# Three edits in an eight-core transformer and state-space kernel: a separate cast, eight weight pieces in a visit, scale factors made per tile

## What is computed

```python
# scan part: x is [2048, 1024] on each core, d_inner 2048, 16 states
xp, z = jnp.split(x @ W_in, 2, axis=-1)
dlt, Bm, Cm = jnp.split(xp @ W_xproj, [64, 80], axis=-1)
delta = jnp.clip(softplus(dlt @ W_dt + b_dt), 0.001, 0.1)
# for every step t: h = (1 + A*dt) * h + (B*dt) * x_t ;  y_t = sum_state(C * h)
y = (scan(xp, delta, A, Bm, Cm) + D * xp) * silu(z)
x = layernorm(x + y @ W_out)
# feed-forward: int8 levels per row for activations, ternary weights
scale_w = 1 / clip(mean(abs(w)), 1e-5);  wq = clip(round(w*scale_w), -1, 1) / scale_w
scale_x = 127 / clip(max(abs(x), axis=-1), 1e-5);  xq = clip(round(x*scale_x), -128, 127) / scale_x
x = layernorm(x + bitlinear(silu(bitlinear(x, w_gate)) * bitlinear(x, w_up), w_down))
```

## Time and profile before

| | |
|---|---|
| runs shown | 9471.68 and 9613.43 us, median 9542.56 |
| the profiled execution | 9519.5 us |
| its span, slowest core (core 2) | 9517.9 us |
| spans of the 8 cores | 9418.7 (core 5) to 9517.9 us |
| VectorE busy | 6221.3 us, 65% of the span |
| TensorE busy | 3550.9 us, 37% |
| ScalarE busy | 1872.1 us, 20% |
| DMA, mean over the span | 68 GB/s |

### The profile page before, as it was taken

The page is one execution under the profiler, slowest core; times in us unless marked ns, Lnnn a source line. Parts: engine busy times, 40 slices in busy tenths (PEclk is TensorE's granted clock), DMA queues, the critical chain, the costliest instruction groups (busy, mean ns, idle before and its releaser), DMA issues.

```text
span 9517.9 us, 48227 instructions; the slowest of 8 cores (9418.7 to 9517.9 us)
## 1 busy us (share of the span) xinstructions
PE 3550.9 (37%) x13683; PEld 1381.4 (15%) x13683; DVE 6221.3 (65%) x4766; ACT 1872.1 (20%) x2102; POOL 0.2 (0%) x4
## 2 busy tenths in 40 slices
PE   6766656999943111111111111100005555222222
PEld 3211112334311000000000000000002222111011
DVE  2555553222144999998879999997774444777776
ACT  0222322111112212112222122211102222111111
POOL 0000000000000000000000000000000000000000
PEclk9655557899865555555555555555557777655556
DMA  3000012111143233333232222222331111000000
GB/s 91 5 0 0 0 40 103 66 54 71 45 157 101 94 91 90 95 84 93 90 99 91 86 82 86 86 84 88 106 120 71 71 71 70 26 27 22 22 27 22
DMA packets 238263, 648.93 MB, mean 68 GB/s; under 512 B 31419, under 2 KB 97196, under 8 KB 230644
## 3 DMA queue, kind: packets, MB, share of 16 engines
q1 hardware_dynamic: 238004, 645.86, 20.6%
HBM read 582.58 MB, written 63.18 MB: 68 GB/s over the span
## 4 chain that ended last, share of the span: by engine, by line
DVE 50%; PE 24%; issue 11%; DMA 7%; ACT 6%; SPq 1%; DVEq 1%; ACTq 0%
DVE b_sl L1219 12%; DVE b_sl L1232 6%; DVE b_sl L1207 6%; DVE qd2B L1444 5%; PE p_hB L694 5%; PE p_eoB L725 4%; DVE ternB L1440 3%; PE p_gA L1665 2%; PE p_uA L1670 2%; DVE rb L443 2%; ACT attbuf L438 2%; DVE zbuf L432 2%; DVE qdD L1444 1%; PE p_mmA L332 1%; PE p_z L447 1%
## 5 line engine op out<-in xcount | busy, mean ns | idle before, releaser
L1219 DVE TENSOR_TENSOR_SCAN b_sl<-a_sl,h_state,b_sl 128x1024 f32<-128x1024 f32 x512 | 1175.8, 2338 | 36.2 <-ACT a_sl L1199 8.8
L1199 ACT ACTIVATE a_sl<-dt_ch,A_all 128x1024 f32<-128x1024 f32 x512 | 559.9, 1140 | 2351.1 <-DVE b_sl L1219 2325.1
L1270 PE MATMUL p_aoC<-wob,ybf 128*128 128x512 bf16 x512 | 167.2, 474 | 1867.8 <-DVE ybf L1251 1769.1
L1232 DVE TENSOR_TENSOR b_sl<-b_sl,bcb 128x2048 f32<-128x2048 f32 x256 | 586.8, 2292 | 28.9 <-DVE h_state L1226 3.2
L1239 DVE TENSOR_TENSOR y_ch<-y_ch,b_sl 128x2048 f32<-128x2048 f32 x256 | 586.8, 2292 | 27.6 <-DVE b_sl L1232 1.4
L1207 DVE TENSOR_TENSOR b_sl<-dxp_ch,bcb 128x2048 f32<-128x2048 f32 x256 | 585.2, 2286 | 18.0 <-DMA bcb<-bc_scr 17.3
L1125 PE MATMUL p_bigC<-x2Tc,wipz 128*128 128x512 bf16 x512 | 146.2, 456 | 1137.9 <-DMA wipz<-win_scr 1137.9
L725 PE MATMUL p_eoB<-w2b,hTe 128*128 128x512 bf16 x2048 | 544.5, 415 | 0.0
L432 DVE SCALAR_TENSOR_TENSOR zbuf<-c_alibi,p_z 128x1024 f32<-128x1024 f32 (+7 forms) x384 | 337.9, 908 | 305.8 <-PE p_z L415 162.0
L694 PE MATMUL p_hB<-xT_hold,w1b 128*128 128x512 bf16 x2048 | 485.0, 404 | 0.5 <-DVE w1b L663 0.3
L1802 PE MATMUL p_trB<-c_ident_bf,qbf2B 128*128 128x128 bf16 x512 | 74.9, 301 | 1052.1 <-DVE qbf2B L1790 952.5
(11 more groups left out here) (196 smaller groups left out, 5559.4 us busy)
## 6 DMA issues: line engine op xcount, KB each, us to landing
bcb<-bc_scr SPq DMA_DIRECT2D x512, 512.0 KB, 4.8
wstgB<-W SPq DMA_DIRECT2D x128, 512.0 KB, 6.1
wstgC<-W_in SPq DMA_DIRECT2D x16, 1024.0 KB, 8.0
x2r<-x_scr SPq DMA_DIRECT2D x32, 512.0 KB, 3.9
wipz<-win_scr SPq DMA_DIRECT2D x256, 64.0 KB, 4.3
wrowD<-w_gate SPq DMA_DIRECT2D x32, 512.0 KB, 3.6
wrowD<-w_up SPq DMA_DIRECT2D x32, 512.0 KB, 3.6
wrowD<-w_down SPq DMA_DIRECT2D x16, 1024.0 KB, 5.2
```

The costliest lines, as they stand in the source:

```text
L1199: amk.append(s.emit("scalar", lambda h, j=j, dc=dc, s_=s_, d=dt2(qp): h.activation(out=a_sl[:, j * TC:(j + 1) * TC], in_=d[:, j * TC:(j + ...
L1219: scn.append(s.emit("vector", lambda h, j=j, dc=dc, s_=s_, bs=bs: h.tensor_tensor_scan(out=bs[:, j * TC:(j + 1) * TC], data0=a_sl[:, j * T ...
L1232: cm = s.emit("vector", lambda h, slot=slot, bs=bs: h.tensor_tensor(out=bs[:].rearrange("p (j t) -> p j t", t=TC), in0=bs[:].rearrange("p ...
```

## The change

There are three edits. In the scan, the multiply by silu(z) writes in place into `y_ch` in f32, and a copy from `y_ch` to `ybf` follows it; the guards take the copy's token, and the wait on `ybf_rd` is gone. In the quantizing loop, eight pieces of the generator are advanced in a visit for five, so the 80 are done after ten tiles. In the down projection, each tile makes its own two factors in two columns of `qcolD2` out of its column of the maxima, where the first tile made them for all.

```diff
@@ end of a quarter, in consume @@
             s.wait("vector", PQ[qi]['zev'])
             s.wait("vector", y_done)
-            s.wait("vector", G['ybf_rd'])
             ymul = s.emit("vector", lambda h, d=zs2(qp): h.tensor_tensor(
-                out=ybf[:], in0=y_ch[:], in1=d, op=ALU.mult))
+                out=y_ch[:], in0=y_ch[:], in1=d, op=ALU.mult))
             G['zs_rd'][qp] = ymul
-            G['y_guard'] = ymul
-            G['dxp_guard'] = ymul
-            ycv = ymul
+            s.wait("vector", ymul)
+            ycv = s.emit("vector", lambda h: h.tensor_copy(out=ybf[:], in_=y_ch[:]))
+            G['y_guard'] = ycv
+            G['dxp_guard'] = ycv
...
             G['wo_guard'] = s.token("tensor")
-            G['ybf_rd'] = G['wo_guard']
@@ end of a visit in the quantizing loop @@
             tr_prev = s.token("tensor")
-            for _ in range(5):
+            for _ in range(8):
                 if next(d0_gen, "end") == "end":
                     break
@@ start of a tile in the down projection @@
-            if tch == 0:
-                s.wait("vector", gmax_done)
-                s2v = s.emit("vector", lambda h: h.tensor_scalar(
-                    out=fu_all[:], in0=gmax_all[:],
-                    scalar1=1.0e-5, scalar2=1.0 / 127.0, op0=ALU.max, op1=ALU.mult))
-                s.wait("vector", s2v)
-                s2r_all = s.emit("vector", lambda h: h.reciprocal(
-                    out=fu_all[:], in_=fu_all[:]))
-            s2r = s2r_all
+            s.wait("vector", gmax_done)
+            s2v = s.emit("vector", lambda h, tch=tch, par=par: h.tensor_scalar(
+                out=qcolD2[:, 2 * par: 2 * par + 1], in0=gmax_all[:, tch:tch + 1],
+                scalar1=1.0e-5, scalar2=1.0 / 127.0, op0=ALU.max, op1=ALU.mult))
+            s.wait("vector", s2v)
+            s2r = s.emit("vector", lambda h, par=par: h.reciprocal(
+                out=qcolD2[:, 2 * par + 1: 2 * par + 2], in_=qcolD2[:, 2 * par: 2 * par + 1]))
...
-                ab2 = s.emit("scalar", lambda h, guh_=guh_, tch=tch, qa2_=qa2_: h.activation(
-                    out=qa2_, in_=guh_, func=AF.Abs, scale=fu_all[:, tch:tch + 1]))
+                ab2 = s.emit("scalar", lambda h, guh_=guh_, par=par, qa2_=qa2_: h.activation(
+                    out=qa2_, in_=guh_, func=AF.Abs, scale=qcolD2[:, 2 * par + 1: 2 * par + 2]))
```

More of the change, by code:

```diff
@@ L971, in build_program @@
                  zs_rd=[None, None], y_guard=None, dxp_guard=None, xp_rd=None,
-                 pbig_free=None, ab0=None, ab1=[None, None], hs_guard=None, ybf_rd=None,
+                 pbig_free=None, ab0=None, ab1=[None, None], hs_guard=None,
                  dltev={}, xdbl={})
```

## The result

The changed kernel takes 9605.12 us (median of 43 runs, 9487.56 to 9716.95); before takes 9540.72 (42 runs, 9442.14 to 9664.74). The ratio of after to before is, over the runs within 1.5% of the fastest and with both halves of the chip alike, 1.0067 with a 95% interval of 1.0036 to 1.0098: about 64 us more, between 34 and 94. The lowest runs of the two differ by 45 us. So the kernel became slower by clearly more than nothing and by less than 2%.

The account below looks back on a forecast made before the run. VectorE carries 50% of the chain that ended last and is on the path at all three edits; TensorE paces the expert layer. 9519.5 + 21.3 + 14 + 0 = 9555 us, range 9485 to 9640.

Parts of the forecast that it names:

- Part A: End of each of 16 scan quarters: one new uncovered f32-to-bf16 copy of 1.33 us, 21.3 us in all, bounds 12 to 38.
- Part B: Quantizing loop, eight weight pieces a visit for five: only waits change, 14 us more, bounds 1 to 37.
- lower bound of 12: Scan: if W_out load waits swallowed the copy in seven of the first eight quarters, 12 us would be left.
- waits for wrowD: Quantizing loop: VectorE's waits for weight pieces grow 8.7 us for w_gate and w_up, fall 3.5 for w_down.
- Abs behind the evacuation, 5 tiles: Quantizing loop, tiles 11 to 15: without pieces as cover, Abs starts 1.12 us late behind ScalarE's evacuation, 5.6 us in all.
- end of the loop: Quantizing loop's exit: the barrier waits for the evacuation instead of the pieces, 8.9 us for 5.6, 3.3 more.
- Part C: Down projection: two small factor steps per tile, about 0.5 us, hidden under late guh reads with 4.5 us to spare; cost 0.
- rival 3: Down projection: the factor steps are not covered and cost 1.9 us in 14 tiles, 27 us more, 9582; chance 0.03.
- rival 1: Quantizing loop: fourth and later w_gate and w_up pieces wait no longer, saving 45 us, 9510; chance 0.07.
- rival 2: Quantizing loop: eight loads push out the x3 load, up to 3.6 us in ten visits, 36 more, 9591; chance 0.05.
- The granted clock of the expert layer (4): Expert layer, before all edits: a clock 0.09 lower on the slowest core makes it over 2% slower, 9745; chance 0.04.

Follow-up runs that it names:

- experiment 1: Only the scan's f32 in-place multiply and copy, in the kernel before: the 15-quarter scan stretch took 3353.5 us against 3330.5.
- experiment 4: Kernel before with eight pieces a visit and each matrix's total emitted with its last piece: quantizing loop 553.5 us, against 560.2 with eight pieces only.
- experiments 5 and 6: Next tile's guh reads issued ahead of the tail's output write, in the kernel before, then also with factors per tile: down projection 1304.8 and 1333.5 us.
- experiment 9: Sixteen weight pieces in a visit for five, in the kernel before, without the other edits: quantizing loop 582.4 us, against 537.8 before.
- experiment 10: Rearranged down projection and four weight slots with early totals together, in the kernel before: 9217.39 to 9350.10 us in 4 runs, ratio 0.972.
- eight alone: Only the eight pieces in a visit for five, in the kernel before: quantizing loop 560.2 us, against 537.8 before.

## Why the prediction was right, and where it was off

It forecast 9555 us, 35 more than the profiled execution of before, all of it from parts A and B. The measured median is 9605. Of these 50 us, 21 are the base: before itself is at 9540.7 in 42 runs, and the sum was made on 9519.5. The other 29 are the size, 64 us for 35. The stretches show 44 to 46 of the 64, so 10 of the 29 are terms of the sum, named below; the last 19 are accounted for by nothing here, and the interval of 34 to 94 holds 35, 45 and 64 alike. The range 9485 to 9640 held the median, and the change is one within 2%. That says little for the sum: the range is 155 us wide because executions differ, with an upper end of 9640 where its own working gives 9648. What bears the forecast out are the stretches and the experiments.

*Part A*, 21.3 us forecast: shown by experiment 1 and the timeline. The row of the same form at another line gave the duration exactly (1227 ns for 1227), and TensorE starts 1.33 us later. The scan stretch with the sixteenth copy grew by 22.7 us with all three edits. The lower bound of 12, by which W_out waits would swallow seven copies, is refuted: VectorE still waits 72.7 us for these loads, for 73.7 in before (8 times each, means of the cores), since they are issued behind a cast that shifts along.

*Part B*, 14 us forecast, 20.4 and 22.4 measured. Term by term, over all eight cores where a mean is given:

| term | forecast | measured |
|---|---|---|
| waits for wrowD | 8.7 - 3.5 = 5.2 | 67.2 to 72.8 us, mean of the cores: 5.6 |
| Abs behind the evacuation, 5 tiles | 5.6 | 4.3 more of the ladder's waits and 5 x 0.2 before the maximum (1.33 for 1.14 us): 5.3 |
| end of the loop | 3.3 | 9.4 - 5.6 = 3.8 |
| first piece of a matrix behind the totals | not in the sum | 2 x 3.1, removed by experiment 4: 6.7 |

The 5.6 us of the first row agree with 5.2 by luck in part. w_gate and w_up cost 6.4 us more (49.1 to 55.5, means of the cores) for 8.7 forecast, and w_down 0.8 less (18.1 to 17.3) for 3.5: both changes were overrated, in opposite directions, and the errors cancel in part.

The step that failed is the sentence "The number of sums, their adds and their loads stays. Only waits can change." Both halves are true, but I went on to price only the waits that before had. The generator issues a fourth kind of instruction, the total per matrix, and a wait on it. That it falls on a visit's border follows from 32 being a multiple of eight and could have been read from the code. By the estimate from the Trainium skill ("DMA: Bandwidth & Descriptors", section "Anatomy of one DMA", a fit for the gpsimd path), 3.2 us to land where the trace of before has 3.6, B would have been 8 us smaller, 6 us. Its waits for wrowD would then have fallen by 3 us where they rose by 5.6; the trace's row was the better price.

*Part C*, 0 us forecast: 1 to 3 measured, nearly within what this stretch does unedited (1400.3 to 1401.7). The cover named for it, SP's late reads of guh, is shown to be the cover by taking it away (experiments 5 and 6): 28.7 us for the 27 of rival 3.

*Rivals.* Cheaper pieces (rival 1): refuted, the waits for w_gate and w_up rose in total. A later piece waited 1.03 us for 1.08 (means over all cores), so strings of eight made it hardly cheaper, and in the longer strings of experiment 9 the single wait rose. The late x3 load (rival 2): x3cD held VectorE for 5.6 us in 2 waits for 3.4 in 2 on the slowest cores (4.1 for 3.4, means of the cores); it did not become a wait of each visit. Uncovered factors (3): not here. The granted clock of the expert layer (4): it moves single executions, as in experiment 10. The slowdown by over 2% that it was to bring did not come; whether it has a part in the 19 us outside the edited stretches, no trace here says.

## What to carry to other kernels

When work is regrouped, list every instruction that its generator emits, the rare ones at borders included, and check where each lands against the new group size: a border that coincides with a group's edge exposes a dependency that was hidden inside it. An edit costed at nothing should have its cover named, and that cover is often an engine's idle time that is itself worth more than the edit: the late reads that hid two small steps a tile here cost 96 us, and rearranging their stage gave back 274, these 96 among them. Where an effect is 0.5% and executions scatter by 2%, compare stretches between the same two instructions on all cores.

## What the runs showed of the hardware

The wait of a late 512 KB load with two buffers in turn is not a constant of the buffers: the fourth and later pieces of a visit waited 1.08 us each in visits of five, 0.98 to 1.03 of eight (eight alone and all three), 1.18 of sixteen (means over all cores), while the median landing by core was 3.6 to 3.8 us in before, 3.3 to 3.7 with eight and 3.5 to 4.2 with sixteen. With four in flight it rose to 4.6 to 5.8 us, and the waits vanished all the same. The scan stretch is the same within 0.6% on all cores and runs (3324 to 3344 us without the copy), whereas the stretch before it ranged from 2891 to 3081 us in the same executions, in which the cores' mean granted clocks were 0.621 to 0.642.
